# Dense weights laid out by the host, loaded in chunks of 128 rows of the contraction, and a first row tile that waits chunk by chunk

## The reference, cut to what matters

```python
x = x + tanh(g_xattn) * autocorrelation(layernorm(x), ctx, ctx)   # 8 heads; FFTs over 512 positions
# autocorrelation: corr = ifft(fft(q) * conj(fft(k))); the 12 largest lags, softmax over them,
#                  out = sum over lags of w * v shifted by the lag (clipped at the end)
x = x + tanh(g_ffn) * ffn(layernorm(x))

def ffn(x):                     # 4096 rows of 2048
    base = x @ W_base.T + b_base                      # W_base: 2048 x 2048
    gate = softmax(x @ W_gate.T)                      # 8 experts
    thr = sigmoid(x @ W_thr + b_thr) / 8
    w = relu(gate - thr); w = w / (sum(w) or 1)
    h = einsum('nd,erd->ner', x, A_w)                 # rank 16 per expert
    return base + 2 * einsum('ner,ne,eor->no', h, w, B_w)
```

## Time and profile before

| what | value |
|---|---|
| time, median of 3 runs | 2907.98 us (2907.73 to 2909.68) |
| time of the profiled execution | 2908.95 us |
| its span | 2907.1 us |
| TensorE busy | 2815.5 us, 97% |
| VectorE, ScalarE, GpSimd busy | 1559.7, 1091.2, 1661.9 us |
| mean of the granted TensorE clock | 0.991 of full |
| moved by DMA | 424.97 MB, mean 146 GB/s |

### The profile page before, as it was taken

The page is one execution under the profiler, slowest core; times in us unless marked ns, Lnnn a source line. Parts: engine busy times, 40 slices in busy tenths (PEclk is TensorE's granted clock), DMA queues, the critical chain, the costliest instruction groups (busy, mean ns, idle before and its releaser), DMA issues.

```text
span 2907.1 us, 35297 instructions
## 1 busy us (share of the span) xinstructions
PE 2815.5 (97%) x12932; PEld 1421.4 (49%) x12932; DVE 1559.7 (54%) x2646; ACT 1091.2 (38%) x1803; POOL 1661.9 (57%) x606
## 2 busy tenths in 40 slices
PE   5999999999999999987999999999999999999999
PEld 2454455555445555546444444444444444444444
DVE  5999999999999999996212112121212121212121
ACT  4666666666666664435211111111112121212110
POOL 4889898989898999950443343434242434333330
PEclk9999999999999999998999999999999999999999
DMA  5444445454444444347555454544444545445441
GB/s 199 131 131 125 131 138 143 145 145 140 121 122 136 134 131 116 102 160 259 167 169 159 148 155 159 152 161 149 159 144 160 152 158 157 153 159 156 148 131 44
DMA packets 264615, 424.97 MB, mean 146 GB/s; under 512 B 156271, under 2 KB 156847, under 8 KB 237109
## 3 DMA queue, kind: packets, MB, share of 16 engines
q1 hardware_dynamic: 245442, 288.93, 33.8%
q10 hardware_dynamic: 19068, 134.73, 13.4%
HBM read 256.79 MB, written 134.32 MB: 135 GB/s over the span
## 4 chain that ended last, share of the span: by engine, by line
PE 52%; DVE 24%; POOL 13%; issue 7%; DMA 2%; ACT 1%; DVEq 0%; ACTq 0%; POOLq 0%
PE bank L1146 42%; DVE top L773 2%; DVE rows_mem L1344 2%; DVE top L782 2%; DVE corr_mem L791 2%; POOL spec_o L916 2%; POOL rows_mem L875 2%; POOL rows_mem L891 2%; POOL v_odd L897 2%; POOL rows_mem L899 2%; POOL rows_mem L892 2%; POOL rows_mem L876 2%; DVE corr_mem L766 1%; PE bank L490 1%; DVE corr_mem L767 1%
## 5 line engine op out<-in xcount | busy, mean ns | idle before, releaser
L1337 DVE TENSOR_TENSOR hwt_lo<-bank,hwt_hi 128x128 f16<-128x128 f32 x32 | 9.3, 292 | 1075.0 <-ACT hwt_hi L1227 1075.0
L1369 POOL TENSOR_TENSOR rows_mem<-norm,rows_mem 128x2048 f16<-128x2048 f32 x31 | 126.1, 4067 | 696.4 <-ACT rows_mem L1208 696.4
L1146 PE MATMUL bank<-w_hi,rows_mem 128*128 128x512 f16 x2048 | 489.3, 379 | 3.8 <-DVE rows_mem L1344 3.8
L1146 PE MATMUL bank<-w_hi,parts_mem 128*128 128x512 f16 x2048 | 489.1, 379 | 3.6 <-DVE rows_mem L1344 3.6
L1227 ACT ACTIVATE hwt_hi<-bank 128x128 f16<-128x128 f32 x32 | 8.9, 277 | 933.8 <-PE bank L1154 908.6
L1146 PEld LDWEIGHTS bank<-w_hi,rows_mem 128*128 128x128 f16 x2048 | 200.4, 98 | 251.5 <-DVE rows_mem L1344 13.7
L1146 PEld LDWEIGHTS bank<-w_hi,parts_mem 128*128 128x128 f16 x2048 | 200.3, 98 | 250.8 <-DVE rows_mem L1344 12.8
L916 POOL TENSOR_TENSOR spec_o<-spec_o,term 128x1024 f32<-128x1024 f32 x127 | 297.7, 2370 | 33.0 <-DVE term L727 28.6
L1146 PE MATMUL bank<-w_lo,rows_mem 128*128 128x512 f16 x1024 | 262.8, 379 | 0.0
L1146 PE MATMUL bank<-w_lo,parts_mem 128*128 128x512 f16 x1024 | 262.8, 379 | 0.0
L490 PE MATMUL bank<-spec_o,table 128*128 128x512 f32 x512 | 251.2, 614 | 10.3 <-POOL spec_o L916 6.3
(11 more groups left out here) (204 smaller groups left out, 5180.6 us busy)
## 6 DMA issues: line engine op xcount, KB each, us to landing
rows_mem<-in_ctx_mirrored_dram SPq DMA_DIRECT2D x32, 1024.0 KB, 9.1
rows_mem<-in_x_mirrored_dram SPq DMA_DIRECT2D x32, 1024.0 KB, 10.4
parts_behind<-parts_mem SPq DMA_DIRECT2D x256, 128.0 KB
parts_ahead<-parts_mem SPq DMA_DIRECT2D x128, 256.0 KB
rows_mem<-x_scratch SPq DMA_DIRECT2D x32, 1024.0 KB, 4.8
rows_mem<-parts_behind ACTq DMA_DIRECT2D x32, 1024.0 KB, 5.9
out_dram<-rows_mem SPq DMA_DIRECT2D x32, 1024.0 KB, 3.9
norm<-in_x_dram ACTq DMA_DIRECT2D x31, 1024.0 KB, 5.8
```

Source lines behind the costliest of these rows:

```text
L1146: mm = pe.matmul(dense[o][:, :], nt(par, part)[:, k, :], w[:, k, o * 512:(o + 1) * 512], start=(k == 0 and n == 0), stop=False)
L1369: pool.tensor_tensor(norm_lo, norm[:, :], norm_hi, ALU.subtract).then_inc(norm_lo_made, 1)
```

## The change

The host lays the dense weights out: W_base transposed (`w_t`), A_w, W_gate and W_thr as one array `ag_t`, already in the shape of the SBUF tile, and B_w as `b_t`. The kernel no longer transposes weights. W comes in 16 chunks of 128 contraction rows. Chunks 0 to 3 go to `rows_mem` in step 31; the others as raw f32 into places of `w_parts` that attention has freed, three places ahead of where their parts will stand (`chunk_place`), so that the high part of chunk n overwrites raw chunk n - 3. Chunk 13 and 15 go to `rows_mem[0]`, chunk 14 into the place of raw chunk 12. Attention's tiles are allocated in another order for this, the spectra split by step parity. ScalarE scales and rounds chunks 0 to 3, the gate weights and B in attention's last steps, GpSimd makes their low parts; chunks 4 to 15 are rounded by ScalarE (`high`) and completed by VectorE (`low`). Of the 20 transposing jobs only the first tile's remains (`turn_first`). base(0) waits for each chunk's low part. The preparation of tile 1 is written out between the chunks. In this cut of the diff, deleted lines stand only where a new line takes their place.

```diff
-                    if NCH <= i < NCH + E:
-                        e = i - NCH
-                        sp.dma_start(b_view[:, :, e, :], b_w[e].rearrange("(n p) r -> p n r", p=128)).then_inc(b_loaded, 16)
+                    if i == NCH:
+                        sp.dma_start(b_rows[:, :], b_t).then_inc(b_loaded, 16)
                     if i == STEPS - 2:
                         first_tile()
+                        sp.wait_ge(v_symmed, 2 * STEPS)
+                        sp.wait_ge(v_joined, 2 * STEPS)
+                        sp.wait_ge(v_made, 4 * STEPS)
+                        sp.dma_start(gated, ag_t.rearrange("p k c -> p (k c)")).then_inc(ag_loaded, 16)
                     if i == STEPS - 1:
                         sp.wait_ge(formed, 2)
                         sp.dma_start(x2_rows[0], norm[:, :]).then_inc(x2_kept, 16)
-                        for m in range(4):
-                            early_weights(m)
+                        for n in range(4):
+                            if n == 2:
+                                sp.wait_ge(ag_lo_made, 1)
+                            sp.dma_start(rows_mem[:, n, :], w_rows[n]).then_inc(chunk_loaded[n], 16)
+                    if i == STEPS:
+                        sp.wait_ge(late_added, 3)
+                        for n in range(4, 8):
+                            sp.dma_start(chunk_place(n), w_rows[n]).then_inc(chunk_loaded[n], 16)
                     if i >= 1:
                         store(i - 1)
...
-                            turn_weights(pe, 0)
+                            turn_first(pe)
...
+                def scale(place, loaded, count, scaled, n):
+                    act.wait_ge(loaded, count)
+                    act.activation(place, place, ACT.Copy, scale=W_SCALE).then_inc(scaled, 1)
+                    act.wait_ge(scaled, n)
+                def early_chunk(n):
+                    act.activation(w_hi[:, n, :], chunk_place(n), ACT.Copy).then_inc(early_hi, 1)
                 def step(i, par, phase):
                     mine, other = X(par), X(1 - par)
                     if i >= 1:
                         copy_w(i - 1, other)
+                    if i == STEPS - 1:
+                        scale(gated, ag_loaded, 16, ag_scaled, 1)
+                        act.wait_ge(q_made, 2 * STEPS)
+                        act.activation(ag_hi.rearrange("p k c -> p (k c)"), gated, ACT.Copy).then_inc(ag_hi_made, 1)
+                        scale(b_rows[:, :], b_loaded, 16, b_scaled, 1)
                     if i == STEPS:
                         deviation_rows(act, 0)
+                        early_chunk(0)
                         normalise_rows(act, 0)
+                        for n in range(1, 4):
+                            scale(chunk_place(n), chunk_loaded[n], 16, chunk_scaled, n + 1)
+                            early_chunk(n)
...
                     if i >= 1:
                         keep_out(i - 1, mine, 1)
+                    if i == STEPS - 1:
+                        scale(chunk_place(0), chunk_loaded[0], 16, chunk_scaled, 1)
+                    if i == STEPS:
+                        first_high(act)
...
+                    if i == STEPS:
+                        early_low(pool, 0)
                     if i >= 1:
...
                         sum_wv(i - 1, 3, 6)
+                    if i == STEPS - 1:
+                        pool.wait_ge(ag_hi_made, 1)
+                        pool.tensor_tensor(ag_lo.rearrange("p k c -> p (k c)"), gated, ag_hi.rearrange("p k c -> p (k c)"),
+                                           ALU.subtract).then_inc(ag_lo_made, 1)
+                    if i == STEPS:
+                        pool.wait_ge(late_added, 3)
+                        for n in range(1, 4):
+                            early_low(pool, n)
...
-            w_hi, w_lo = sb("w_hi", [128, KD, D], f16), sb("w_lo", [128, KD, D], f16)
+            w_parts = sb("w_parts", [128, KD, 2, D], f16)
+            w_hi, w_lo = w_parts[:, :, 0, :], w_parts[:, :, 1, :]
+            def chunk_place(n):
+                if n < 4 or n in (13, 15):
+                    return rows_mem[:, n if n < 4 else 0, :]
+                return w_parts[:, 15 if n == 14 else n + 3].rearrange("p a c -> p (a c)").bitcast(f32)
             parts16, corr16 = parts_mem[:, :].bitcast(f16), corr_mem[:, :].bitcast(f16)
-            nt_mem = parts16[:, 0:2 * D].rearrange("p (a k t) -> p a k t", a=2, k=KD)
+            nt_mem = corr16.rearrange("p (a k t) -> p a k t", a=2, k=KD)
             ag_hi, ag_lo = (parts16[:, 2 * D + n * KD * NG:2 * D + (n + 1) * KD * NG].rearrange("p (k c) -> p k c", k=KD)
                             for n in range(2))
-            b_hi, b_lo = corr16[:, 0:D], corr16[:, D:2 * D]
+            b_hi, b_lo = parts16[:, 0:D], parts16[:, D:2 * D]
...
             def sync_dense(sp):
+                sp.wait_ge(out_made, 2 * STEPS)
+                for n in range(8, 13):
+                    sp.dma_start(chunk_place(n), w_rows[n]).then_inc(chunk_loaded[n], 16)
+                sp.wait_ge(early_lo, 1)
+                sp.dma_start(chunk_place(13), w_rows[13]).then_inc(chunk_loaded[13], 16)
+                for n in (14, 15):
+                    sp.wait_ge(wt_lo, n - 5)
+                    sp.dma_start(chunk_place(n), w_rows[n]).then_inc(chunk_loaded[n], 16)
+                sp.wait_ge(b_lo_made, 1)
                 sp.dma_start(bias[:, :], b_base.rearrange("(a n) -> a n", a=1).to_broadcast([128, D])).then_inc(small_loaded, 16)
                 sp.dma_start(thr_b[:, :], b_thr.to_broadcast([128, 1])).then_inc(small_loaded, 16)
...
-                sp.wait_ge(wt_made, 2 * JOBS)
+                sp.wait_ge(wt_lo, KD - 4)
                 load(0)
                 for i in range(ROWS):
                     step(i, i % 2)
...
+            def turn_first(pe):
+                pe.wait_ge(normed, 1)
                 for h in range(2):
                     for k in range(8):
                         d = (8 * h + k) * 128
+                        mm = pe.transpose(first_banks(h)[:, k, :], norm[:, d:d + 128], ident[:, :])
+                    mm.then_inc(first_turned, 1)
+            def first_high(act):
+                for h in range(2):
+                    act.wait_ge(first_turned, h + 1)
+                    act.activation(nt_mem[:, 0, 8 * h:8 * h + 8, :], first_banks(h), ACT.Copy).then_inc(first_hi, 1)
+            def first_low(dve):
+                for h in range(2):
+                    dve.wait_ge(first_hi, h + 1)
+                    dve.scalar_tensor_tensor(out=nt_mem[:, 1, 8 * h:8 * h + 8, :], in0=first_banks(h), scalar=1.0,
+                                             in1=nt_mem[:, 0, 8 * h:8 * h + 8, :], op0=ALU.mult, op1=ALU.subtract)\
+                       .then_inc(first_lo, 1)
+            def early_low(pool, n):
+                pool.wait_ge(early_hi, n + 1)
+                pool.tensor_tensor(w_lo[:, n, :], chunk_place(n), w_hi[:, n, :], ALU.subtract).then_inc(early_lo, 1)
...
                 def base(i, par):
                     for k in range(KD):
+                        if fmost(i) == 0 and k < 4:
+                            pe.wait_ge(early_lo, k + 1)
+                        elif fmost(i) == 0:
+                            pe.wait_ge(wt_lo, k - 3)
                         for n, (part, w) in enumerate(((0, w_hi), (0, w_lo), (1, w_hi))):
...
                 def experts(i):
+                    if fmost(i) == 0:
+                        pe.wait_ge(b_lo_made, 1)
                     pe.wait_ge(hwt_hi_made, i + 1)
                     pe.wait_ge(hwt_lo_made, i + 1)
...
-                pe.wait_ge(wt_hi, 2 * JOBS)
-                pe.wait_ge(wt_lo, 2 * JOBS)
+                pe.wait_ge(ag_lo_made, 1)
+                pe.wait_ge(first_lo, 2)
                 logits(0, 0)
+                pe.wait_ge(out_kept, 2 * STEPS)
                 tiles(pe, step)
...
+                def high(n):
+                    act.wait_ge(chunk_loaded[n], 16)
+                    if n >= 7:
+                        act.wait_ge(wt_lo, 11 if n == 15 else n - 6)
+                    act.activation(w_hi[:, n, :], chunk_place(n), ACT.Copy, scale=W_SCALE).then_inc(wt_hi, 1)
+                def high_b():
+                    act.wait_ge(parts_stored, 192 * STEPS)
+                    act.activation(b_hi, b_rows[:, :], ACT.Copy).then_inc(b_hi_made, 1)
...
                 load_norm(1)
+                for n in range(4, 8):
+                    high(n)
                 load_sine(1, 1)
+                for n in range(8, 12):
+                    high(n)
+                high_b()
                 keep_x2(1, 1)
+                high(12)
+                deviation_rows(act, 1)
+                high(13)
+                normalise_rows(act, 1)
+                rounded(1, 1)
+                high(14)
+                high(15)
                 tiles(act, step)
...
                 def step(i, par):
                     gating(i)
+                    if fleast(i) >= 1 and fmost(i) + 1 < ROWS:
```

(14 more changed lines are left out.)

145 lines of the change are left out of this document (40 added, 105 removed).

## The result

The changed kernel takes 2889.97 us (median of 4 runs, 2888.23 to 2890.60) against 2907.86 us (4 runs, 2906.80 to 2909.68): 17.9 us less, a ratio of 0.9937 with a 95% interval of 0.9921 to 0.9953. The forecast was 2878.5, 29.5 us less. The measured time lies 11.5 us above it: inside the stated range of 2864 to 2892, but outside rival A's own 2869 to 2886, and the rival value nearest to it is D's 2891.5. The profiled execution took 2889.89 us, its span 2888.1.

What follows compares the result with a forecast made beforehand. TensorE, busy 97% of the span, was taken as the bound, the gain being what base(1) moves: 1430.1 to 1400.6 (T 1381 + 0.5 + 11 + 5.5 + 2.6), 29.5 us less. Forecast 2878.5 us, range 2864 to 2892.

Steps and rivals of the forecast that it cites:

- rival A: The forecast itself: 2878.5 us, its own range 2869 to 2886; chance 0.56.
- D: Queue rival: eleven loads of the chunk stream at 4.0 us each, T at 1394, time 2891.5; chance 0.13.
- Attention: Attention's last steps: added ScalarE and GpSimd work fits into idle time, cost 0, ending at 1317.9 as before.
- The stream: Chunk loads after attention: 2.8 us per load, 8.5 for the stores; chunk 8 lands at 1343, chunk 11 at 1354.3.
- B: Clean-stream rival: T at its lower bound of 1371, gain 39.5 to 44.4 us, time 2863.6 to 2868.5; chance 0.13.
- E: Slower rival: the stream at the stores' rate throughout, 4.1 us more a load, 45 in all, 2923.5; chance 0.04.
- The conversion: Chunks' high parts 1.9 us on ScalarE, low parts 2.3 on VectorE, which wait for running GpSimd operations; last ends at 1381.
- T: End of the last chunk's low part (chunk 15), forecast at 1381, lower bound 1371; base(1) was put at T + 19.6.
- The transposes: Tile 1's two DMA transposes start after T behind load(0): 11 us, plus 0.5 for load(0).
- Tile 2 keeps all of base(1), 41 us, for its own preparation.: Behind base(1): later tiles follow each other as before, so the gain is what base(1) moves.
- C: Clock rival: base(0) at 1.2 GHz from chunk 8 on, ending 1388.5, base(1) at 1403, time 2881; chance 0.10.
- F: Late chunks make starting base(0) by chunk worth nothing, the removed 60 us only spent waiting: 2905; chance 0.04.

Runs made afterwards that it cites:

- e1: Changed kernel with tile 1's two DMA transposes issued before SP's wait for the last low part, load(0) after them: 2880.21 us.
- e4: Changed kernel with GpSimd's low part of B replaced by a memset, its product left out of the output: 2884.53 us.
- e5: Changed kernel with the x load of tile 2 held back until tile 1's transposes have landed: 2889.94 us.
- e6: Changed kernel with both the x load of tile 2 and load(0) held back until tile 1's transposes have landed: 2893.32 us.
- e9: e1 plus ScalarE's rounding of tile 1's gates, hw_hi(1), moved ahead of tile 3's sine load: 2873.51 us.
- e10: e5 plus ScalarE's rounding of tile 1's gates, hw_hi(1), moved ahead of tile 3's sine load: 2880.45 us.
- e7: Changed kernel with ScalarE's x and cosine loads of tile 1 issued only after the high part of chunk 8: 2895.24 us, one run.
- e2: Changed kernel with base(0) waiting once for all chunks' low parts, instead of one wait per chunk: 2911.46 us.
- e3: Changed kernel with chunks 8 to 13 issued ahead of the last stores in SP's queue: 2889.62 us.
- e12: e9 plus B's high part ahead of chunk 8's, and B's low part between tile 1's two sums on GpSimd: 2871.85 us.

## Why the forecast was right in direction and 11.5 us too fast

**Attention.** Held: its last matmuls ended 0.3 us later than before, GpSimd's early low part (1294.3, 4.1 us) was over before the sums. These began at 1299.39, later than the 1299.1 that I had named as a sign of being wrong, but GpSimd had stood idle for 0.95 us waiting for VectorE, so the low part did not hold them. logits(0) and base(0) started at 1318.0 and 1320.9, forecast 1318 and 1321, at full clock.

**The stream.** Chunk 8: forecast 1343, here 1348.9. The longest wait was to be at chunks 14 and 15; it was here, 14.7 us against 5.4. It is a spread rather than a value: in e1, e4, e5, e6, e9 and e10, whose code is the same up to there, it landed between 1343.3 (e9) and 1348.7 (e1). The term that was mis-sized is what lies ahead of it. I gave the loads the rate of loads alone, 378 GB/s, and the stores 8.5 us. Where both were in the queues only 308 GB/s flowed. That is shown; how much of the delay is due to the two loads of ScalarE is not: e7 gives 4.6 to 10.4 us for them, against the 5.6 of the forecast. Loads beside stores and loads alone are two prices. Between them, up to 18.8 us from issue to landing say only how full the queues were: chunk 14, alone, took 4.9. Rivals B (a clean stream) and E (the stores' rate throughout) both fall.

**The conversion.** The mechanism was right and its size too small for this execution. (The prediction says that without the exclusion its sum would be about 5 us shorter. By its own terms it is about 2: 1.0 at chunk 12's low part, behind B's, and 1.1 at chunk 14's, behind the remainder.) I charged GpSimd's operations near chunk 12 and left the low parts of chunks 8 to 11 at 2.3 us; they took 6.9 us more in the changed kernel. In the balance this and the late landing overlap: the low part of chunk 11 ended at 1366.9, forecast 1358.5, and 1.2 us of that came back, as B's low part no longer met chunk 12's. From the end of chunk 12's low part to T it took 15.7 us, forecast 16.1. T was 1387.8 instead of 1381. In e1, e2, e5, e6, e9 and e10, with the same code on VectorE and GpSimd up to there, T was 1382.6, 1381.6, 1382.2, 1385.3, 1384.6 and 1380.9: the order in which the two engines get hold of what they share comes out differently from one to the next (the low parts of chunks 9 to 11 took 13.46 us from 1350.28 in e9 and 8.87 from 1350.19 in e10). The middle of these six is 1382.4, 1.4 behind the forecast, so the forecast of T fits the other kernels and not this one. Why is open. The forecast had no term for such a spread; but T is known for one execution of the changed kernel only, and its four times lie within 2.4 us of each other, which speaks against a T that moves by 5 us between them.

The Trainium skill (SBUF — State Buffer, section "Who interferes with whom") says that issue order decides which of the two engines blocks, for the whole instruction, and that a GpSimd instruction that only writes SBUF doesn't contend with a VectorE one of two SBUF inputs. Both agree with the traces: low parts of 4.45 us beside the remainder, a sum of 6.29 us behind a low part, and in e4 no loss beside the memset.

**The transposes.** The step that failed most plainly: "both DMA transposes start after T", and for them "I take 11". I priced them from single ones, 4.4 and 7.4 us, at 11 us and 0.5 for load(0). But two loads of 1.05 MB follow from the same event T: load(0), which stands in SP's queue ahead of them, and the x load of tile 2, issued 1.0 us behind them, which the sum doesn't have at all. Issued at 1388.3 the transposes ended at 1405.5, T + 17.7 instead of T + 11.5. e5, e10 and e6 are the proof: beside load(0) alone they end near T + 10, within the 11.5, and with no load beside them they take 6.9. So what failed is the term for the x load of tile 2, put at nothing. The question that I had not put to the trace is what else starts at T.

**logits(1) and the experts** took 7.1 us, not 8.1: the granted clock was 0.50 (1.2 GHz) from 1404 to 1407 and 0.74 on average from 1407 to 1411, so part of them ran at 2.4 GHz. Sum at base(1): 6.8 + 6.2 - 1.0 + 0.1 = 12.1 us late. Behind it came 1.7 back, since in the kernel before the experts of tile 1 had waited 1.5 us for the gates' low part.

**"Tile 2 keeps all of base(1), 41 us, for its own preparation."** hw_hi(1), ScalarE's rounding of tile 1's gates, sits behind both sums of tile 3, and these follow from T through the x load of tile 2. In the changed kernel it ran at 1455.18, 0.3 us after the gates were turned. In e3 and e4, which keep this order, base(1) started at 1408.9 and 1405.8, no expert matmul of tile 1 waited, and the profiled executions are shorter than the changed kernel's by just what base(1) moved, 3.8 and 6.9 us. So the sum "what base(1) moves is the gain" holds down to 1405.8 at least. It fails in e1, where base(1) started at 1393.05 (a wait of 6.60 us), and in e5, at 1400.05 (7.22 us), where the held x load makes the rounding late as well; both then ran experts that take 2.6 us at the full clock partly at the half one. The forecast's own case, T 1381 and base(1) at 1400.6, was never run. An estimate: the rounding ran 62.2 us behind T in e1 and 66.2 in e4, so it could run at 1443 to 1447, and the experts 0.8 behind it; they are wanted 45 to 46 us behind the start of base(1) (e5, e1), at 1446 to 1447. That is a wait of 0 to 2 us, so this step alone would have cost the forecast little. e9 and e10 show that the queue's order is what bounds the kernels in which base(1) starts earlier.

**Rivals.** C (clock) didn't bite: during the long wait for chunk 8 the granted clock was 0.50, 1.2 GHz (1351 to 1356), and the 36 matmuls behind it took 10.28 us, but the next low part was later still (0.20 us of waiting), so nothing hung on it. D (4.0 us a load throughout; its 2891.5) has the value nearest to the measured time, but by a T of 1394 that didn't come; where loads lay beside stores such a price may hold (e7: 2.3 to 5.2 us a load), but there alone. F is out by e2.

That the time fell inside the range owes something to luck. The range reaches up to 2892 only by D, whose mechanism was not at work throughout; the x load was missing from the sum, and the 1.7 us that came back behind base(1) were not in it either.

What stays open: why T was 5 us later in the changed kernel than in the middle of the other six; why the x load costs more beside the transposes (7.6 us) than its bytes do at 378 GB/s; what the two loads in front of chunk 8 cost; and what part of the stores' slowness is their shape. None of these was measured alone.

## What to carry to other kernels

When a wait is broken into pieces, the gain ends where the next queue order has its slack, so look one or two tiles downstream for an instruction that stands behind another tile's work: here the moved rounding of the gates gave 5 to 10 us in each of the three kernels in which base(1) started early. Holding one transfer back to speed up another can make that later instruction late (e5). Price a transfer by what its releasing event also releases, and by the mix in the queue, not by a single one elsewhere in the trace. An operation that keeps the neighbouring engine waiting should be free in a gap in which that engine has nothing to do; the one test of it, e12, gave 1.7 us, inside the scatter.

## What the runs showed of the hardware that I had not expected

- VectorE's two-operand SBUF operation and GpSimd's hold each other in both directions: 2.29 us became 4.45 behind a running GpSimd operation (1379.00), 4.5 became 6.29 and 6.59 behind a running VectorE one (changed kernel, e9). A GpSimd memset (1.80 us) held nobody.
- Two DMA transposes of 0.5 MB each: 6.9 us for both alone (e6), 9.6 and 9.5 beside one load of 1.05 MB (e5, e10), 16.0 to 21.3 beside two (changed kernel, e3, e4, e7), in the changed kernel 17.2 at a DMA share of 1.06 and 183 GB/s.
- At a DMA share of 0.98 (1330 to 1340) the issuing engine took longer over its issues too: SP needed 9.8 us for five chunk loads (1330.1 to 1339.9), 1.1 to 3.1 us each, against 0.4 to 0.7 us each for chunks 4 to 7 (1313.3 to 1315.3), before which no DMA was running.
- The same code up to T gave T between 1380.9 and 1387.8 in seven kernels, each profiled once: where two engines contend for what they share, one trace is one draw. Whether one kernel's executions differ as much wasn't measured.
